# First attention layer of a two-layer kernel on one core: every engine's order within a step written out anew

## What is computed

```python
# first layer, attention: 16 heads of 8 features, context of 128 rows per sequence
x = x + _L0_xattn_ref(_layernorm(x), ctx_1024, ctx_1024, mask_BxS2_bf1, Wq, bq, Wk, bk, Wv, bv, Wo, bo)
    scores = jnp.einsum('bnlh,bnph->bnlp', qm, km) / np.sqrt(HEAD_DIM)
    attn = jax.nn.softmax(jnp.where(mask, scores, MASK_FILL), axis=-1)
    out = jnp.einsum('bnlp,bnph->bnlh', attn, vm)          # then @ Wo.T + bo
# first layer, feed-forward: 8 experts, each row goes to the 2 with the largest logits
x = x + _L0_ffn_ref(_layernorm(x), w_gate, w1, w2)
# second layer: 16 heads of 64 features, then a plain feed-forward part
x = x + _L1_xattn_ref(_layernorm(x), ctx_1024, mask_BxS_ik0, Wq, Wkv, Wout, bout)
x = x + _L1_ffn_ref(_layernorm(x), w1, b1, w2, b2)
```

## Time and profile before

| | us |
|---|---|
| median of 3 runs | 1075.23 (1074.84 to 1075.88) |
| the profiled execution | 1078.77, its span 1076.9 |
| of it, from start to the first sequence's addition to X (L857) | 42.6 |
| from the first to the 32nd addition to X | 371.7 |
| all that comes behind | 662.6 |

### The profile page before, as it was taken

How to read it: one execution, slowest core, us unless ns; L and a number is a source line. 1 busy time by engine, 2 the same in 40 slices (tenths; PEclk the granted TensorE clock), 3 DMA queues, 4 the chain that set the end, 5 groups by cost and what they waited for, 6 DMA issues and landing times. The chain is left out here.

```text
span 1076.9 us, 30219 instructions
## 1 busy us (share of the span) xinstructions
PE 942.5 (88%) x8590; PEld 805.1 (75%) x8590; DVE 671.6 (62%) x2173; ACT 596.2 (55%) x2537; POOL 416.6 (39%) x670
## 2 busy tenths in 40 slices
PE   5888788888888873799995799999999999999987
PEld 3556566555665652799995688999999999999986
DVE  5667767767777666122222667777777777777763
ACT  2867777767777670133331455556555655555552
POOL 4123333333333333011113455555555555555531
PEclk9989999989999895799997899999999999999998
DMA  5764475554754522122222011111111111111110
GB/s 152 223 196 148 132 234 163 181 151 132 232 167 139 149 93 62 44 69 68 69 68 71 30 56 51 45 56 59 59 56 56 59 41 52 59 59 59 56 45 9
DMA packets 110658, 103.56 MB, mean 96 GB/s; under 512 B 11759, under 2 KB 96563, under 8 KB 110614
## 3 DMA queue, kind: packets, MB, share of 16 engines
q1 hardware_dynamic: 102958, 89.14, 26.9%
q0 software_dynamic: 5776, 12.99, 3.8%
q10 hardware_dynamic: 1880, 0.92, 0.3%
HBM read 56.45 MB, written 46.56 MB: 96 GB/s over the span
## 5 line engine op out<-in xcount | busy, mean ns | idle before, releaser
L580 ACT ACTIVATE PR<-bank,nmx 128x128 f32<-128x128 f32 x1024 | 362.4, 375 | 130.3 <-issue 114.5
L580 ACT ACTIVATION_READ_ACCUMULATOR PR<-bank,nmx 128x1 f32 x1024 | 218.4, 213 | 0.0
L748 DVE TENSOR_REDUCE nmx<-bank 128x4 f32<-128x512 f32 x256 | 170.0, 685 | 69.8 <-PE bank L1045 60.4
L316 POOL TENSOR_TENSOR PR<-PR,rden 128x512 f32<-128x512 f32 x128 | 134.0, 1047 | 92.5 <-DVE rden L753 91.5
L1027 PE MATMUL bank<-ident,PR 128*128 128x128 f32 x1024 | 152.5, 277 | 0.3 <-DVE YT L759 0.3
L1027 PEld LDWEIGHTS bank<-ident,PR 128*128 128x128 f32 x1024 | 121.0, 143 | 29.9 <-issue 25.9
L1192 PE MATMUL bank<-XCT,wqk 128*128 128x128 f32 x1024 | 123.8, 281 | 0.9 <-ACT XCT L572 0.9
L1192 PEld LDWEIGHTS bank<-XCT,wqk 128*128 128x128 f32 x1024 | 120.6, 197 | 1.6 <-ACT XCT L572 1.6
L572 ACT ACTIVATE XCT<-bank 128x256 f32<-128x256 f32 x64 | 24.7, 385 | 160.9 <-PE bank L1019 160.9
L1074 PE MATMUL bank<-wv,XCT 128*128 128x512 f32 x128 | 74.2, 663 | 37.9 <-ACT wide L595 37.9
L649 ACT ACTIVATE H<-bank 128x512 f32<-128x512 f32 x70 | 41.9, 598 | 107.5 <-PE bank L1162 107.5
(11 more groups left out here) (178 smaller groups left out, 1810.2 us busy)
## 6 DMA issues: line engine op xcount, KB each, us to landing
second_layer_values<-wide SPq DMA_DIRECT2D x32, 512.0 KB, 2.8
wide<-second_layer_values SPq DMA_DIRECT2D x32, 512.0 KB, 3.3
expert_outputs<-HF SPq DMA_DIRECT2D x32, 256.0 KB
expert_outputs<-HF SPq DMA_DIRECT2D x64, 128.0 KB
KBD<-expert_outputs SPq DMA_DIRECT2D x128, 64.0 KB
QS<-expert_outputs SPq DMA_DIRECT2D x32, 256.0 KB
PR<-expert_inputs SPq DMA_DIRECT2D x36, 128.0 KB, 2.1
expert_outputs<-PR POOLq DMA_DIRECT2D x35, 128.0 KB, 2.0
```

The costliest lines, as they stand in the source:

```text
L316: nc.gpsimd.tensor_tensor(unit, unit, rden[:, p, G * g:G * g + G].unsqueeze(2).broadcast_to([P, G, P]), ALU.mult).then_inc(s["nm"], 1)
L580: last = nc.scalar.activation(PR[:, g, j * P:(j + 1) * P], S_BANK[g % 2][:, j * P:(j + 1) * P], ACT.Exp, bias=nmx[:, p, h:h + 1], accum_ou ...
L748: nc.vector.tensor_reduce(nmx[:, p, G * g:G * g + G], S_BANK[g % 2][:].rearrange("p (j k) -> p j k", j=G), AXX, ALU.max, negate=True).then ...
```

## The change

Every engine's `step0` in the first part lists its operations in another order. The operations are the same, with the same operands, except for sequence numbers. Seen from the scores of a sequence:

- ACT: between the first and the second group of exponentials stands the reading of the first half of the second layer's values (before: behind both groups and behind the copy `PARTS[:, 2]`). That copy (signal `qh`) goes to between the third and the fourth group. The copy of this layer's values goes to the step's end as before, but of values computed behind the next step's first scores.
- PE: the step begins with `values`, of sequence n-2 instead of n-1. This is the same place in the row of scores (behind group 3 of one step, ahead of group 0 of the next). Behind them stand the transposes of group 1, of `XND` and of group 2, and only then the output projection. This layer's values are projected behind the first scores. The transpose of `RB` goes from just ahead of the last scores to behind the keys' and queries' projection.
- DVE: `QC` comes last of the four operations that follow the keys' projection, and the low query part (`PARTS[:, 3]`, signal `ql`) goes to the next step, behind `OT0`. The addition to `X` follows at once, ahead of the first row maximum. `XND`'s scaling goes to behind the third row maximum, and its transposed copy to the next step.
- POOL: the copy to `XK` goes from the end of a step (behind the scatter) to the next step's beginning, behind `RB`.
- SP: the context is loaded first, and the values are stored ahead of the query parts. ACT's and SP's steps now run to 35, and ACT's loop begins at step 4 like the others'. `late_loads` stay between the same loops, behind the query parts' stores and ahead of the next `KBD` loads.

The diff, cut; first SP and POOL:

```diff
-                    wait_apart(sp, (a["qw"], 32 * (m + 1)))
-                    sp.dma_start(QS[:, 1 - p, :, :].bitcast(FP32),
-                                 spread(1 - p, 0).rearrange("(g x) s -> x g s", g=NU)).then_inc(a["qs"], 16)
+                q = 1 - p
                 if exists(n + 3):
-                    load_ctx(sp, a, n + 3, 1 - p)
+                    load_ctx(sp, a, n + 3, q)
                 if isinstance(n, int):
                     early_loads(n)
...
+                    wait_apart(sp, (a["qw"], 32 * (n + 2)), (a["s"], NU * (n)))
+                    sp.dma_start(QS[:, q, :, :].bitcast(FP32),
+                                 spread(q, 0).rearrange("(g x) s -> x g s", g=NU)).then_inc(a["qs"], 16)
...
-                    wait_apart(sp, (a["ql"], m + 1), (a["qs"], 16 * (m - 1)))
+                if exists(n + 1):
+                    wait_apart(sp, (a["pjv"], 2 * (n + 2)))
+                    sp.dma_start(v_dram[n + 1], V_OUT).then_inc(a["vst"], 16)
+                if exists(n + 2):
+                    wait_apart(sp, (a["ql"], n + 3), (a["qs"], 16 * (n + 1)))
                     for o in range(2):
                         sp.dma_start(spread(p, 0).rearrange("(c o i) s -> o c i s", o=2, i=2)[o],
                                      PARTS[:, 2 + o, :].unsqueeze(1).broadcast_to([P, 2, P])).then_inc(a["qw"], 16)
-                if exists(n + 1):
-                    wait_apart(sp, (a["pjv"], 2 * n + 4))
-                    sp.dma_start(v_dram[n + 1], V_OUT).then_inc(a["vst"], 16)
...
+                if exists(n - 3):
+                    wait_apart(pool, (rt["xn"], n - 2), *([(rt[f"sc{q}"], 2 * loads(n - 5, q))] if exists(n - 5) else []))
+                    nc.gpsimd.tensor_copy(XK[:, q, :], XND[:]).then_inc(rt["kept"], 1)
...
+                        nc.gpsimd.indirect_dma_start(xs, bass.IndirectOffsetOnAxis(scat_idx[:, p, k:k + 1], 0), XK[:, p, :],
                                                      None).then_inc(rt[f"sc{p}"], 16)
-                if exists(n - 2):
-
-                    wait_apart(pool, (rt["xn"], n - 1), *([(rt[f"sc{p}"], 2 * loads(n - 4, p))] if exists(n - 4) else []))
-                    nc.gpsimd.tensor_copy(XK[:, p, :], XND[:]).then_inc(rt["kept"], 1)
```

ACT:

```diff
-                    read_xct(a, l, p, True, a["v0"], l - 1)
+                q = 1 - p
+                if exists(n + 2):
+                    read_xct(a, n + 2, p, True, a["v0"], n + 1)
                 if exists(n):
                     exponentials(a, n, p, 0)
+                if exists(n + 1):
+                    read_v_half(n + 1, 0)
+                if exists(n):
                     exponentials(a, n, p, 1)
-                if exists(l):
-
-                    act.wait_ge(a["qc"], l + 1)
-                    wait(act, a["qw"], 32 * l)
-                    nc.scalar.activation(PARTS[:, 2, :].bitcast(FP32R), QC, ACT.Copy).then_inc(a["qh"], 1)
-                if exists(m):
-                    read_v_half(m, 0)
                 if exists(n - 1):
                     read_PT(a, n - 1, 3)
-                if exists(n):
-                    exponentials(a, n, p, 2)
+                if exists(n + 1):
+                    read_v_half(n + 1, 1)
                 if exists(n - 1):
                     act.wait_ge(a["rt"], n)
                     wait(act, a["oN"], n - 1)
                     nc.scalar.activation(RTS[:], M2_BANK[:, 2 * P:3 * P], ACT.Copy).then_inc(a["rts"], 1)
-                if exists(m):
-                    read_v_half(m, 1)
+                if exists(n):
+                    exponentials(a, n, p, 2)
+                if exists(n + 2):
+                    act.wait_ge(a["qc"], n + 3)
+                    wait(act, a["qw"], 32 * (n + 2))
+                    nc.scalar.activation(PARTS[:, 2, :].bitcast(FP32R), QC, ACT.Copy).then_inc(a["qh"], 1)
                 if exists(n):
                     exponentials(a, n, p, 3)
                     read_PT(a, n, 1)
-                if exists(m):
-                    act.wait_ge(a["v0"], m + 1)
-                    wait(act, a["pv"], NU * (m - 1))
-
```

DVE, the places that are spoken of:

```diff
+                if exists(n + 1):
+                    dve.wait_ge(a["qh"], n + 2)
+                    wait(dve, a["qw"], 32 * (n + 1))
+                    nc.vector.tensor_tensor(PARTS[:, 3, :].bitcast(FP32R), QC, PARTS[:, 2, :], ALU.subtract).then_inc(a["ql"], 1)
+                if exists(n - 3):
+                    dve.wait_ge(rt["tr"], n - 2)
+                    wait(dve, rt["lg"], n - 3)
+                    nc.vector.tensor_copy(XDT[:], M_BANK[:, 0:P]).then_inc(rt["xct"], 1)
...
+                if exists(n - 2):
+                    dve.wait_ge(a["o"], n - 1)
+                    xrow = X[:, bass.ds(n - 2, 1), :].rearrange("p o d -> p (o d)")
+                    nc.vector.tensor_tensor(xrow, M2_BANK[:, 0:P], xrow, ALU.add).then_inc(a["x"], 1)
...
-                    dve.wait_ge(a["kq"], l + 1)
-                    nc.vector.scalar_tensor_tensor(KC, bank[4][:, 0:P], bqk[:, 1:2], mk_bc[:, bass.ds(l * P, P)],
-                                                   ALU.add, ALU.mult).then_inc(a["kc"], 1)
-                    wait(dve, a["qh"], l)
-                    nc.vector.tensor_scalar(QC, bank[4][:, P:2 * P], float(DH0) ** -0.5, bqk[:, 0:1],
-                                            ALU.mult, ALU.add).then_inc(a["qc"], 1)
...
-                    dve.wait_ge(a["qh"], l + 1)
-                    wait(dve, a["qw"], 32 * l)
-                    nc.vector.tensor_tensor(PARTS[:, 3, :].bitcast(FP32R), QC, PARTS[:, 2, :], ALU.subtract).then_inc(a["ql"], 1)
...
+                if exists(n + 2):
+                    dve.wait_ge(a["kq"], n + 3)
+                    nc.vector.scalar_tensor_tensor(KC, bank[4][:, 0:P], bqk[:, 1:2], mk_bc[:, bass.ds((n + 2) * P, P)],
+                                                   ALU.add, ALU.mult).then_inc(a["kc"], 1)
...
+                    nc.vector.tensor_tensor(PARTS[:, 1, :].bitcast(FP32R), KC, PARTS[:, 0, :], ALU.subtract).then_inc(a["kl"], 1)
+                    dve.wait_ge(a["kq"], n + 3)
+                    wait(dve, a["qh"], n + 2)
+                    nc.vector.tensor_scalar(QC, bank[4][:, P:2 * P], float(DH0) ** -0.5, bqk[:, 0:1],
+                                            ALU.mult, ALU.add).then_inc(a["qc"], 1)
+                if exists(n):
+                    row_max(a, n, p, 2)
...
+                if exists(n - 2):
+                    norm_alone_apply(dve, rt, n - 2)
...
-                if exists(n - 1):
-                    dve.wait_ge(a["o"], n)
-                    xrow = X[:, bass.ds(n - 1, 1), :].rearrange("p o d -> p (o d)")
-                    nc.vector.tensor_tensor(xrow, M2_BANK[:, 0:P], xrow, ALU.add).then_inc(a["x"], 1)
```

PE:

```diff
+                if exists(n - 2):
+                    wait(pe, a["pt0"], upto(n - 2, 2, 1))
+                    wait(pe, a["pt1"], upto(n - 2, 2, 1))
+                    wait(pe, a["vc"], upto(n - 2))
+                    wait(pe, a["qc"], upto(n + 1))
...
+                    values(n - 2, p)
+                if exists(n - 1):
+                    transpose_unit(a, n - 1, 1)
+                if exists(n - 3):
+                    pe.wait_ge(rt["xn"], n - 2)
...
+                    nc.tensor.transpose(M_BANK[:, 0:P], XND[:], ident[:]).then_inc(rt["tr"], 1)
+                if exists(n - 1):
+                    transpose_unit(a, n - 1, 2)
+                if exists(n - 2):
+                    pe.wait_ge(a["oN"], n - 1)
...
+                    mm(M2_BANK[:, 0:P], OT0[:, p, :], wo0T[:], start=True, stop=False)
+                    mm(M2_BANK[:, 0:P], ones3[:], brow[:, 1, :], start=False, stop=True).then_inc(a["o"], 1)
+                if exists(n):
+                    scores(n, p, 0)
...
+                    pe.wait_ge(a["xct"], n + 1)
+                    wait(pe, a["oN"], upto(n - 2))
...
+                    mm(bank[4][:, 2 * P:3 * P], XCT[:, p, 1, :], wv0T[:], start=True, stop=False)
+                    mm(bank[4][:, 2 * P:3 * P], ones3[:], brow[:, 0, :], start=False, stop=True).then_inc(a["v0"], 1)
...
+                if exists(n + 2):
+                    wait(pe, a["x"], upto(n - 2))
...
+                    transpose_in(a, n + 2, p, True)
...
+                if exists(n - 1):
+                    pe.wait_ge(a["rb"], n)
+                    wait(pe, a["xct"], upto(n + 2))
...
+                    nc.tensor.transpose(M2_BANK[:, 2 * P:3 * P], RB[:], ident[:]).then_inc(a["rt"], 1)
...
-                if exists(n - 1):
-                    wait(pe, a["rb"], n)
...
-                    nc.tensor.transpose(M2_BANK[:, 2 * P:3 * P], RB[:], ident[:]).then_inc(a["rt"], 1)
-                if exists(n):
                     scores(n, p, 3)
-                if exists(n - 1):
-                    values(n - 1, q)
-                if exists(n):
-                    transpose_unit(a, n, 1)
...
-                    mm(bank[4][:, 2 * P:3 * P], XCT[:, q, 1, :], wv0T[:], start=True, stop=False)
```

(5 more changed lines are left out.)

236 lines of the change are left out of this document (118 added, 118 removed).

## The result

The changed kernel takes 1004.11 us in the median of 4 runs (1000.26 to 1007.77), the kernel before beside it 1075.46. The ratio is 0.9337, with a 95% interval of 0.9298 to 0.9375. The profiled execution took 1007.77 us, its span 1006.1.

A forecast was written before the change was run, and what follows sets the result against it. A ring of waits between PE and ACT, no full engine, was the bound. Regular steps 36.7, disturbed 6.7, first 0.7 and last four 3.5 us made 47.6 off 1078.77: 1031.2 profiled, 1028 median; range 1006 to 1060.

The forecast's parts named there:

- a ring of waits: PE and ACT each wait for the other once per step in the first part; one round 11.65 us, no engine full.
- The ring cut short: PE-ACT round in the first part loses 1.52, 0.39 and 0.49 us, from 11.65 to 9.25 us.
- The 1.00 us of transposes to cover OT0: Transposes behind the values' matmuls fill the 1.00 us left until PE may go on, removing its 0.49 us wait.
- The regular step: Undisturbed step of the first part: from 11.82 to 10.15 us, with PE's own work next to bound it.
- hand-overs: PE waits for ACT just in time at three places in a step, 0.1 us each: 0.3 us.
- The second ring: Two groups of exponentials, reading a half, last scores, values, OT0, then DVE to the first row maximum: 9.0 to 9.5 us.
- The disturbed steps: Four longer steps in the first part, some 11.5 us above regular ones; excess kept, each gaining as regular steps do: 6.7 us.
- two effects cancelling: In disturbed steps, POOL's late norm no longer holds up DVE (11.5 us gone), but QS can be late by as much.
- the way of the query parts through DRAM: Store and load of the query parts before their scores: 6.4 us needed, 3.7 us remaining, no cost in regular steps.
- The ends: First step 0.7 us less, last four steps 3.5 us less (bounds 0 and 7); the start and all that follows stay.
- PE isn't full: Rival: PE's busy time is no bound, so the step falls to 9.3 us; 1005 us in all; chance 0.13.

## Why the prediction was off

**What bounded the kernel** was read rightly: a ring of waits, not a full engine. PE's wait for ACT's reading is gone, as are PE's for OT0 and most of ACT's for the transposed input; putting one move back brings the first of them back.

**The ring cut short** was put at 9.25 us. With the first half alone left late the step is 10.29, and the part taken off the ring by reading it early was put at 1.52; that would give 8.8, below what bounds the step now. The single move was worth 1.2 and 0.9 us in the runs, less than 1.52; in both PE's wait for ACT's reading was gone with it, and another bound came in between. The 1.00 us of transposes to cover OT0 was right: the output projection starts 2.96 us behind the values' matmuls, 2.90 was forecast.

**The regular step** is the step that failed. It was taken as PE's busy time of 9.86 us plus 0.3 for hand-overs, 10.15; it is 9.38. Both terms were wrong. PE's busy time for the same work fell from 9.67 and 10.05 us to 9.29 and 9.30, so part of it was waiting that the trace counts as busy, and it was no floor. By the run with two more transposes PE's own work is at most 9.25. And there were no costs of hand-overs: the trace marks no wait of PE in a regular step. What sets the step in PE's place is the DVE ring, at 9.38. Of the 23.4 us by which the profiled execution lies below the forecast of 1031.2, this step of the prediction is 26 x 0.77 = 20.0.

The Trainium skill (Perfetto Trace Analysis, section Identifying the Most-Contended Engine) says that matmul busy time isn't a good measure of how close PE is to its roofline, and that the weight loads' busy time and the share of peak FLOPs are to be used. That it errs upward, as the prediction put it, is the prediction's own reading; it held here, with 9.86 us against at most 9.25. The weight loads, 6.89 us in the step of 11.51, rightly left room, but 7.18 in the step of 9.38 doesn't tell how far the step could fall. The rival built on this had a step of 9.3 and 1005 us. Its step was right; that its total came within 1 us is partly luck, since it had 65 us for the 26 steps and 5 for the ends, and they gave 55.3 and 11.6, with 3.8 of scatter behind them. Nor was PE far from full: it was busy for 9.29 of 9.38 us. The rival was given 0.13, on an argument (11.65 less PE's waits leaves 10.0) that took all the time outside the marked waits for PE's own work.

**The second ring** was put at 9.0 to 9.5 us, by way of the first row maximum. What holds the step is a near relative of it, through OT0, the addition to X, the transposes of the input and the second row maximum; at 9.38 us it is within that range, but this ring was not named.

**The disturbed steps** were taken as unchanged in what they have above a regular one, 11.5 us, with two effects cancelling. Both occurred. POOL's wait fell by 56 us, and the two disturbed steps at the start are gone (27.34 to 8.85 + 9.57). But QS is late behind four of SP's groups of loads, which is 57.96 - 4 x 9.38 = 20.4 us. The 26 steps together went from 318.87 to 263.53 us, 55.3 less; 26 times 2.44 is 63.4, so 8.1 us were given back. The forecast for them was 43.4. In regular steps the way of the query parts through DRAM cost nothing, as said.

**The ends.** The first step lost 0.73 us, as forecast (0.7), but by chance: in the changed kernel's second profile it is 10.80 us, not 10.14. The last four lost 11.6 us (41.93 to 30.29), not 3.5: the forecast gave them a share of the regular gain, but with less work each they drop below it, to 8.97, 8.70, 8.22 and 4.40 us, the last being one in which no scores are left, since the values' matmuls now come a step later. The bound of 7 was too narrow. What lies behind X of the last sequence went from 662.6 to 658.9 us of span, with no edit in it; a second profile of the kernel before has 658.9 there, so this is scatter. In the sum, from the start, the first step, the 26 steps, the last four, what lies behind, and the time outside the span: 0.7 - 0.7 - 55.3 - 11.6 - 3.8 - 0.2 = -71.0 us.

**The range** ended at 1006 because half of the rival "PE isn't full" was left out of it, and the step fell to that rival's length.

## What to carry to other kernels

Before PE's busy time is taken as the floor of a step, add up the distances from start to start of its groups where nothing waits, or add a small known piece of work and see what the step does: here 0.22 us on PE cost 0.09, 0.20 on DVE cost 0.20, and a copy on ACT nothing. Then look for the place where the step took the added time: the 0.09 was a wait of DVE for logits behind the added transposes, and not a full PE. When a tuned step gets shorter, loads that one queue issues in a block between steps begin to be felt; cut into pieces, one or two between two steps, the same bytes left the steps at 9.38 here, and the whole took 12.7 us less. And a comparison of variants is worth little without the reference variant on the same chip: two runs that seemed to show costs of 0.6 and 0.8 us showed the chip.
